# A four-attention chain in float32: one attention's query weights folded into its keys, masks and the maximum's subtraction on DVE, eps inside the statistics

## The reference, cut to what matters

```
x = block0(x): layernorm, attention with 8 heads of 32, residual; layernorm, U = (.. @ W_in.T + b_in) @ B
               s = silu(s @ A.T) + u_t over the 1024 rows; x += states @ C; x += mod
x = block1(x): qn = layernorm(x)*g + b;  q = qn @ wq + bq;  k, v = layernorm(ctx) @ wkv + bkv   (16 heads of 64)
               attn = softmax(causal(q k^T / 8));  x = attn v @ wo + bo + x
x = block2(x): q = x @ Wq.T + bq; scores = q k^T / 4                                            (16 heads of 16)
               scores = where(mask == 0, -1e9, scores); e = exp(scores - max) * mask
               probs = e / (sum(e) + 1e-9); x = layernorm(probs v @ Wo.T + bo + x)
x = block3(x): layernorm, scores = where(xa_mask, -float_max, q k^T / 4), softmax, @ v, proj    (16 heads of 16)
               x += attention; x += gelu(layernorm(x) @ fc1 + b) @ fc2 + b
```

## Time and profile before

| | |
|---|---|
| median of 3 runs | 1515.07 us (1514.07 to 1515.09) |
| the profiled execution | 1518.26 us, its span 1516.3 us |
| granted TensorE clock, mean | 0.984 |
| PE, PEld | 1438.1 us (95%), 1238.9 us (82%) |
| DVE | 954.2 us (63%) |
| ACT | 678.0 us (45%) |
| POOL | 451.6 us (30%) |

### The profile page before, as it was taken

How to read it: one execution, slowest core, us unless ns; L and a number is a source line. 1 busy time by engine, 2 the same in 40 slices (tenths; PEclk the granted TensorE clock), 3 DMA queues, 4 the chain that set the end, 5 groups by cost and what they waited for, 6 DMA issues and landing times.

```text
span 1516.3 us, 25350 instructions
## 1 busy us (share of the span) xinstructions
PE 1438.1 (95%) x9947; PEld 1238.9 (82%) x9947; DVE 954.2 (63%) x2220; ACT 678.0 (45%) x1507; POOL 451.6 (30%) x755
## 2 busy tenths in 40 slices
PE   6897888999999999999999999999999999899999
PEld 5776777888789879888897898878986998699778
DVE  4776664088756766586658627775677557747772
ACT  3554655523444344534454552345434443453443
POOL 4365442021431232134123311151115212420341
PEclk9999999899999999999999999999999999999999
DMA  3151233020000000000000001000000000000000
GB/s 94 46 115 45 82 82 114 1 75 1 1 16 8 8 2 15 15 1 7 9 15 1 8 15 16 2 1 8 22 1 1 15 15 1 1 15 15 1 1 14
DMA packets 46738, 34.22 MB, mean 23 GB/s; under 512 B 21981, under 2 KB 45340, under 8 KB 46108
## 3 DMA queue, kind: packets, MB, share of 16 engines
q1 hardware_dynamic: 46571, 32.59, 7.7%
q10 hardware_dynamic: 48, 0.01, 0.0%
HBM read 23.26 MB, written 8.39 MB: 21 GB/s over the span
## 4 chain that ended last, share of the span: by engine, by line
PE 85%; DVE 6%; ACT 4%; POOL 3%; issue 1%; DMA 1%; ACTq 0%; SPq 0%; DVEq 0%; POOLq 0%
PE ps L697 13%; PE ps L772 10%; PE ps L769 9%; PE ps L814 8%; PE ps L748 8%; PE ps L822 7%; PE ps L729 7%; PE ps L782 5%; PE ps L733 4%; PE ps L681 4%; PE ps L739 3%; PE ps L894 2%; PE ps L912 1%; DVE mx L1179 1%; ACT pr L1012 1%
## 5 line engine op out<-in xcount | busy, mean ns | idle before, releaser
L1391 POOL TENSOR_SCALAR rstd<-mv 128x1 f32<-128x1 f32 x192 | 43.1, 225 | 635.0 <-DVE mv L1152 634.2
L1012 ACT ACTIVATE pr<-pr 128x616 f32<-128x616 f32 x224 | 159.7, 716 | 156.5 <-DVE pr L1189 106.3
L1179 DVE TENSOR_REDUCE mx<-ps 128x8 f32<-128x616 f32 x224 | 178.0, 795 | 81.2 <-PE ps L739 47.5
L1016 ACT ACTIVATE pr<-ps 128x512 f32<-128x512 f32 x224 | 131.9, 595 | 189.7 <-PE ps L748 189.2
L991 ACT ACTIVATE tt<-ps,cols 128x128 f32<-128x128 f32 x320 | 127.5, 455 | 161.7 <-PE ps L681 160.7
L1248 DVE TENSOR_TENSOR xt<-xt,ps 128x256 f32<-128x256 f32 x192 | 79.9, 418 | 163.6 <-PE ps L822 83.0
L748 PE MATMUL ps<-ident,pr 128*128 128x128 f32 (+1 forms) x1120 | 162.4, 279 | 9.8 <-ACT pr L1012 5.6
L697 PE MATMUL ps<-tt,wq 128*128 128x128 f32 x1280 | 158.9, 278 | 2.7 <-ACT tt L991 2.5
L772 PEld LDWEIGHTS ps<-vtab,pr 128*128 128x128 f32 (+1 forms) x1280 | 153.5, 192 | 9.6 <-ACT pr L1016 7.3
L697 PEld LDWEIGHTS ps<-tt,wq 128*128 128x128 f32 x1280 | 152.2, 194 | 6.9 <-ACT tt L991 4.3
L772 PE MATMUL ps<-vtab,pr 128*128 128x34 f32 (+2 forms) x1280 | 153.8, 271 | 4.0 <-ACT pr L1016 3.5
(11 more groups left out here) (182 smaller groups left out, 2302.4 us busy)
## 6 DMA issues: line engine op xcount, KB each, us to landing
out_dram<-xt SPq DMA_DIRECT2D x64, 128.0 KB, 1.7
xt<-in_x_dram SPq DMA_DIRECT2D x32, 128.0 KB, 2.3
xt<-out_dram SPq DMA_DIRECT2D x32, 128.0 KB, 2.1
fc<-in_L_xattn_fc_w_dram SPq DMA_DIRECT2D x2, 1024.0 KB, 6.9
big<-in_L_xattn_wkv_dram SPq DMA_DIRECT2D x1, 2048.0 KB, 11.3
front<-in_L_xattn_wkv_dram SPq DMA_DIRECT2D x1, 2048.0 KB, 7.9
wo<-in_L_xattn_wo_dram SPq DMA_DIRECT2D x1, 1024.0 KB, 5.7
wq<-in_L_xattn_wq_dram SPq DMA_DIRECT2D x1, 1024.0 KB, 4.9
```

The lines of the kernel that those rows point to most:

```text
L1012: ac(v, v, ACT.Exp, scale=-ATTN[key[0]].scale).then_inc(done["expo"], 1)
L1016: ac(pr[:, run.lane, 0:4 * P], bank(run.lane, 0), ACT.Copy).then_inc(done["pturn_main"], 1)
L1179: v.tensor_reduce(mx[:, run.lane, :], score_view(run.lane), AX.X, ALU.max).then_inc(done["rowmax"], 1)
```

## The change

Five things are changed together, and the written order of all engines with them.

1. `L1`: the query is not made any more. A table `wk` [256 x 16 heads x 77 keys] for each batch of the pair takes its place: (layernorm gain and query weights) x keys, made by PE once per pair (`wk_mm`) and copied by DVE (`wk_sb`). Gain, bias `b` and `bq` go into it: the normalized row has its first column dropped (the columns sum to zero) and a column of ones added. The scores of a group are then four matmuls of 308 columns, two for each bank. The weights are prepared once (`fold` on POOL, `wqt_mm` on PE, `wqt_sb` on ACT). `query_add` is gone for this attention, and its `turned` is one plain copy of 256 columns.
2. `L2`, `L3`: PE adds no masks. DVE reads the scores from PSUM, adds the mask (`L3`, from the bytes of the mask) or takes the minimum with a bound (`L2`), and writes to `pr` (`bound`); `rowmax` reads `pr`, and `below` subtracts in SBUF. Two DVE steps become three.
3. eps times 256 stands as a third statistic in `stat`, so `aggr` gives var + eps, and `vareps` is gone.
4. POOL makes `mul2` and a `bound2`, and not `neg3`, nor the zeros of `kblk1`.
5. `big` is halved; the first half of the MLP's hidden columns goes into `pr`. The pair-0 value tables `vtw` have room for both groups.

```diff
 def norm_steps(key):
-    return [("stats", key), ("aggr", key), ("vareps", key), ("rstd", key), ("norm", key)]
+    return [("stats", key), ("aggr", key), ("rstd", key), ("norm", key)]
 def attention_steps(a):
-    if a is L1:
-        steps = [("query", "1a"), ("query", "1b"), ("query_add", "1a"), ("query_add", "1b")]
+    steps = [] if a is L1 else [("query", a.name), ("query_bias", a.name)]
...
-        steps += [("scores", k), ("rowmax", k), ("shift", k), ("expo", k)]
+        steps += [("scores", k)]
+        steps += [("bound", k), ("rowmax", k), ("below", k)] if a in (L2, L3) else [("rowmax", k), ("shift", k)]
 TURNS = {
     "tensor": (
-        "1010132031210310213002322312101301010201321013031030232120301231231301202013101301032032213210230131320310201212"
+        "0101023130013010121200213213210320210121303210100121323230310302020123211010321302320212310123013232102301013210301"
...
             def scores(key, run):
+                if a is L1:
+                    for k in range(2):
+                        h0 = (g * HG + k * HB) * KEYS
+                        for kc in range(KC):
+                            last = mm(bank(lane, k)[:, SFROM[k]:SFROM[k] + HB * KEYS], t[:, lane, kc, :], wk[:, kc, b, h0:h0 + HB * KEYS],
+                                      start=kc == 0, stop=kc == KC - 1 and run.tile > 0, skip_group_check=True)
...
-                if masked:
-                    m = {"1": causal[:, :, :], "2": neg2[:, run.tile:run.tile + 1, :],
-                         "3": neg3[:, run.batch, run.tile:run.tile + 1, :]}[a.name]
-                    for k in range(2):
-                        last = mm(bank(lane, k)[:, SFROM[k]:SFROM[k] + HB * KEYS], identb[:, :], m.to_broadcast([P, HB, KEYS]),
-                                  start=False, stop=True, skip_group_check=True)
+            def wqt_mm(key, run):
...
+                for kc in range(KC):
+                    last = mm(bk[:, 0:H], wq1[:, kc, c * P:(c + 1) * P], fold1[:, kc, :], start=kc == 0, stop=kc == KC - 1)
+            def wk_mm(key, run):
...
+                for n, c in enumerate(WK_PARTS[part]):
+                    for k in range(2):
+                        half = slice(k * P // 2, (k + 1) * P // 2)
+                        last = mm(item_bank("wk_mm", key, pair, k)[:, n * PK:(n + 1) * PK], wqT[half, c, ec * P:(ec + 1) * P],
+                                  kT[c // GC][half, c % GC, :], start=True, stop=True)
-            def query_add(key, run):
+            def bound(key, run):
+                dve.wait_ge(done["scores"], at("scores", key, run))
...
+                if key[0] == "2":
+                    top = bound2[:, run.tile:run.tile + 1, :].to_broadcast([P, HG, KEYS])
+                    last = v.tensor_tensor(heads_view(run.lane), score_view(run.lane), top, ALU.min)
+                else:
+                    off = out3[:, run.batch, run.tile:run.tile + 1, :].to_broadcast([P, HG, KEYS])
+                    last = v.scalar_tensor_tensor(heads_view(run.lane), off, NEG, score_view(run.lane), ALU.mult, ALU.add)
+            def below(key, run):
+                dve.wait_ge(done["rowmax"], at("rowmax", key, run))
+                top = mx[:, run.lane, :].unsqueeze(2).to_broadcast([P, HG, KEYS])
+                v.tensor_tensor(heads_view(run.lane), top, heads_view(run.lane), ALU.subtract).then_inc(done["below"], 1)
+            def wk_sb(key, run):
...
+                for k in range(2):
+                    o = wk[:, ec, :, :].rearrange("p b (c k n) -> p b c k n", k=2, n=KEYS)[:, :, c0:c0 + n, k, :]
+                    src = item_bank("wk_mm", key, pair, k)[:, 0:n * PK].rearrange("p (c b n) -> p b c n", c=n, b=PAIR)
+                    last = v.tensor_copy(o, src)
-            def vareps(key, run):
             def do_rstd(key, run):
-                pool.wait_ge(done["vareps"], at("vareps", key, run))
+                pool.wait_ge(done["aggr"], at("aggr", key, run))
             def do_masks(key, run):
...
-                    made(p.tensor_scalar(neg3[:, :, :, :], m3raw, NEG, None, ALU.mult))
...
+                made(p.tensor_scalar(bound2[:, :, :], mul2[:, :, :], 0.0, NEG, ALU.is_equal, ALU.mult))
+                p.tensor_scalar(bound2[:, :, :], bound2[:, :, :], -NEG, -1e9 / L2.scale, ALU.add, ALU.add).then_inc(done["masks"], 1)
```

More of the change, by code:

```diff
@@ L120, in table_steps @@
     p = str(pair)
-    steps = [] if pair else ([("v0_lay", p)] + [("weights_get", i) for i in range(LOADS)] + [("wkv1_get", p), ("masks", "2"), ("masks", "3")])
+    steps = [] if pair else ([("v0_lay", p)] + [("weights_get", i) for i in range(LOADS)] + [("wkv1_get", p), ("masks", "2")])
     if pair == 0:
@@ L124, in table_steps @@
             steps += [("w2_mm", str(i)), ("w2_sb", str(i))]
+        steps += [("fold", "1")]
+        for c in range(L1.chunks):
+            steps += [("wqt_mm", str(c)), ("wqt_sb", str(c))]
     else:
@@ L129, in table_steps @@
         steps += [("k_mm", f"{p}1{c}"), ("k1_sb", f"{p}1{c}")]
-    for g in range(L1.groups):
-        for c in range(GC):
-            steps += [("vt_mm", f"{p}{g}{c}"), ("vt_sb", f"{p}{g}{c}")]
-        for b in range(PAIR):
-            for j in range(TILES):
-                steps += [("vwo_mm", f"{p}{g}{b}{j}"), ("vwo_sb", f"{p}{g}{b}{j}")]
+    folded = []
+    for ec in range(KC):
+        for part in range(3):
+            folded += [("wk_mm", f"{p}{ec}{part}"), ("wk_sb", f"{p}{ec}{part}")]
+    values = [[(s, f"{p}{g}{c}") for c in range(GC) for s in ("vt_mm", "vt_sb")] for g in range(L1.groups)]
+    products = [[(s, f"{p}{g}{b}{j}") for b in range(PAIR) for j in range(TILES) for s in ("vwo_mm", "vwo_sb")] for g in range(L1.groups)]
+    if pair == 0:
+        steps += values[0] + values[1] + folded + products[0] + products[1]
+    else:
+        steps += folded + values[0] + products[0] + values[1] + products[1]
     for a in (L2, L3):
@@ L156 @@
     "tensor": ("turn", "query", "scores", "pturn", "mix", "proj", "uproj", "ssm", "fc1", "fc2",
-               "w2_mm", "k_mm", "vt_mm", "vwo_mm", "v_mm", "scan_u", "scan_r", "gap_turn", "more_pe"),
-    "scalar": ("turned", "query_bias", "expo", "pturn_main", "u_sb", "gelu", "w2_sb", "k1_sb", "vt_sb", "silu", "more_act"),
-    "vector": ("stats", "aggr", "norm", "query_add", "rowmax", "shift", "rowsum", "den_eps", "recip", "weigh",
-               "pturn_rest", "heads", "resid", "resume", "vwo_sb", "k_sb", "v_sb", "ends", "gap", "agree", "states"),
-    "gpsimd": ("vareps", "rstd", "prebias", "keep", "maskmul", "gain", "offset", "masks", "vtw_zero"),
+               "w2_mm", "wqt_mm", "k_mm", "wk_mm", "vt_mm", "vwo_mm", "v_mm", "scan_u", "scan_r", "gap_turn", "more_pe"),
+    "scalar": ("turned", "query_bias", "expo", "pturn_main", "u_sb", "gelu", "w2_sb", "wqt_sb", "k1_sb", "vt_sb", "silu", "more_act"),
+    "vector": ("stats", "aggr", "norm", "bound", "rowmax", "below", "shift", "rowsum", "den_eps", "recip", "weigh",
+               "pturn_rest", "heads", "resid", "resume", "wk_sb", "vwo_sb", "k_sb", "v_sb", "ends", "gap", "agree", "states"),
+    "gpsimd": ("rstd", "prebias", "keep", "maskmul", "gain", "offset", "masks", "fold", "vtw_zero"),
     "sync": ("load", "put", "get", "store", "weights_get", "wkv1_get", "v0_lay", "v_lay")}
@@ L239, in in_turn, with places @@
     assert all(at[c] == len(own[c]) for c in PLANS), engine
+    return out
+RING = ((2, 3, 4, 5, 6, 7), (0, 1, 2, 3))
+WK_PARTS = ((0, 1, 2), (3, 4, 5), (6, 7))
+def places(pair):
+    out, n = {}, 0
+    for s, k in table_steps(pair):
+        if s.endswith("_mm"):
+            n += n % 2 if s == "wk_mm" else 0
+            out[s, k] = n
+            n += 2 if s == "wk_mm" else 1
     return out
@@ L417, in xattn_chain @@
         mm_no = {it: n + 1 for n, it in enumerate(ITEMS)}
-        RING = ((2, 3, 4, 5, 6, 7), (0, 1, 2, 3))
-        EMPTIES = {"w2_mm": "w2_sb", "vt_mm": "vt_sb", "vwo_mm": "vwo_sb", "v_mm": "v_sb"}
-        TMM = [[(s, k) for s, k in table_steps(pair) if s.endswith("_mm")] for pair in range(2)]
+        EMPTIES = {"w2_mm": "w2_sb", "wqt_mm": "wqt_sb", "wk_mm": "wk_sb", "vt_mm": "vt_sb", "vwo_mm": "vwo_sb", "v_mm": "v_sb"}
+        PLACES = [places(pair) for pair in range(2)]
         def emptied(step, key):
@@ L706, in scores @@
                     if a is L1:
[L707 to L708 removed]
+                        pe.wait_ge(done["turned"], at("turned", "1", run))
                     else:
```

366 lines of the change are left out of this document (199 added, 167 removed).

## The result

The changed kernel took **1533.53 us** (median of 18 runs, 1520.12 to 1543.08); the kernel before, run beside it, 1516.96 (18 runs, 1511.02 to 1528.22). The ratio is 1.0083, with a 95% interval from 1.0053 to 1.0112: 0.8% slower, where 4.2% faster was forecast. The longest of the 18, over 1.5% above the shortest, counts as a slow run and is left out of the ratio; without it the median is 1533.22 us. The medians alone stand 1.1% apart, so a difference of medians here is good to some 3 or 4 us.

What follows compares the result with a forecast made beforehand. The prediction took PE to bound the kernel, busy 95% of the span, with DVE next in phase 1. Its terms took 1518.3 us to 1455.0, less 3.2: about 1452 us; own range 1435 to 1470, 80% range 1412 to 1492.

Steps and rivals of the forecast that it cites:

- signs that the prediction named: Listed checks: PE instruction count, step prices, DVE busy time, PE share, phase 1 length, largest POOL piece near 105 us.
- length of phase 1: Phase 1 of a pair was to take 525 to 545 us in place of 560 and 590.
- folding, tables, epsilon, stall, table loads: L1 query -113.7, wider scores +63.5, new PE tables +18.6, scan-end stall -3.9, POOL tables -3, vareps -5.4, ACT loads +3 us.
- masks leave PE: L2 and L3 in phase 1: 256 mask matmuls at 185 ns go, 47.4 us counted in full.
- bounds come on DVE: Phase 1: DVE gains net 66.8 us of work; +25 us taken on the path, between 0 and 46.
- PE waits for little: Phase 1: PE is busy 97 to 98%, so its -97.6 us of query, masks and scores counts in full.
- rival D: Removing masks and query pays nothing, as PE's short steps only filled its waits: 1515 +- 3 us; chance 0.03.
- waits for DVE: Phase 1: chain time on DVE, 91 us, grows as DVE's idle share falls from 33 to 22%; +25 us taken.
- rival B: DVE's waits grow more than its idle share says: +58 in place of +25 us, so 1485 us; chance 0.20.
- Rival C: DVE becomes the bound in phase 1: slower, 1621 us, if its share stays below about 73%; chance 0.07.
- weight loads don't set the pace: PE's matmul time follows columns: 128 and 256 columns, one load each, cost 111 and 216 ns; no term rests on it.
- small terms: Among them: vareps gone -5.4 us, stall at the scan's end -3.9, mask tables on POOL -3.

Runs made afterwards that it cites:

- searched orders: Phase 1 orders from a search over a replay of each kernel's trace: before 1509.5 us, changed 1512.5 and 1500.5, changed with masks back on PE 1470.9.
- zeros added there: Changed kernel with the 256 mask matmuls put back on PE as adds of zero, DVE's bounds kept: 1545.0 us, ratio 1.0180.
- the fastest kernel: Changed kernel with the L2 and L3 masks back on PE and a searched order of phase 1: 1470.9 us, ratio 0.9685 to the kernel before.

## Why the prediction was wrong

The prices of single steps were right, and almost all signs that the prediction named came out: 1120 instructions less, 260 ns for the wide scores, 0.79 and 0.87 us on DVE, DVE at 1020 us and 67% (1035 and 71% forecast), 2.32 us for the largest new POOL piece, now at 116 us (under 3 forecast), PE at 93% (93 to 95). What failed is the length of phase 1, about 560 and 594 us (932 to 1526) in place of 525 to 545, and with it the sum. By parts, in us:

| part | forecast | in the change's order | in searched orders |
|---|---|---|---|
| folding, tables, epsilon, stall, table loads | -41 | +2.6 | -38.6 |
| masks leave PE | -47.4 | -17 (of the kernel before) | -18.3 |
| bounds come on DVE | +25 | +30 (estimate) | +48 to +60 |
| all | -63 | +15.6 | -9.0 to +3.0 |

(The first row is -113.7 + 63.5 + 18.6 - 3.9 - 3 - 5.4 + 3. Measured: 1520.5 - 1517.9; 1470.9 - 1509.5. Second row: the kernels without masks. Nobody left the masks out in the change's order, so its -17 is taken from the kernel before, and the +30 that hangs on it is an estimate; zeros added there cost 11.5, which would make it +25. Third row: 1533.5 - 1520.5 + 17; 1500.5 or 1512.5 less 1452.7.)

**The step that failed** is "PE waits for little. Hence I count it in full, and put what is late next into the terms for waits". A busy share of 97 to 98% says that PE is seldom idle, not that taking work away from it brings the end nearer. Two kernels give 0.36 and 0.39 of a mask matmul's time. That the next step in the written order isn't ready any earlier is the likely reason; the runs show only the share. The masks alone make 30 of the 80 us between forecast and result. So nearly two thirds of the masks' time went as in rival D (the steps only filled PE's waits), to which I gave 0.03.

**The folding** made 44 more. The forecast's sum for it was met to 3 us (-41 against -38.6), but only between two orders that were both chosen for their kernels. That closeness is luck in part: the searches are good to some 12 us, a mask in the same order paid only 0.39 of its length, and the 43.8 us of `query_add` on DVE, which go with the query, were in the forecast's waits and not in this sum. How the 38.6 us divide isn't shown. In the order that came with the change the folding brought nothing. I took the change's order as given and asked of it only what stands where. A written order is a set of guesses on who is ready when; steps that grow from 136 to 260 ns a matmul, and others that vanish, can make them stale. What in the change's order loses the 40 us isn't shown: it wasn't tried with the folded kernel in the order of before, whose tables have other banks.

**The waits for DVE** were sized about right in the change's order (+25 against an estimated 25 to 30); DVE's part of the chain went from 91 to 137 us, the upper end of my range. In a tight order they cost 48 to 60 us for 101 us of bounds, as rival B priced them (+58), and more than the 18 that PE saves: the masks are better on PE in every order tried. Rival C named the outcome, slower, and its sign: DVE's share of phase 1 reached 70% (802.2 of 1140 us), under its 73%. Its mechanism isn't borne out. With the masks back on PE in the same order DVE has 63% (708.5 of 1133) and the time is 13 us less, where C had about 100.

**The clock** was no term at all, and no rival. Of the 80 us it has about 33: the changed kernel runs 104 us longer at 1.2 GHz than the kernel before (147 against 43), at 0.32 each. That is an estimate, since the price is the slope over 18 runs. It isn't a part beside the others, but lies in all measured rows above: the folded kernel with the masks on PE had 73 us there, in its new order 35. Summed over PE's steps of phase 1 in the two profiled executions, the time above a step's usual length is 55.0 us after and 8.3 before, so 47 us of the busy time that didn't go. The Trainium skill, "TensorE: Matmul & The Clock Gate", section Terms, puts the loss at the time at the lower level times one half; for the 104 us that would be 52, an estimate by that page. PE's steps agree with it: in the two stretches PE was at the lower level for some 115 us after (clock 0.97 and 0.93) and some 17 before, and 47 is about half of the difference. The time of the whole kernel doesn't, with 0.32 in place of 0.5; that part of the loss falls into waits is likely and not shown. Waits and clock may feed each other: from 1155 us PE waits in a stretch at full clock, and then does its transposes in 1.33 instead of 0.55 us. The order in time is shown, the cause isn't.

The claim that weight loads don't set the pace, on which no term rested, holds (260 ns with one load each). The small terms held in part where they can be seen: epsilon -5.3; at the scan's end the stall isn't gone, four ACT pieces of 0.4 us are left from 296.6 us, as the one shown, in place of 3.9 us; and where GpSimd makes the mask table, now from 115 to 121 us, PE is busy 11.48 of the 14 us from 112, in place of 9.73 of 14, so 1.8 us more, against 3 forecast.

## What to carry to other kernels

Where engines follow a written order, ask of a matmul that goes not how long it is, but what stands behind it and whether that is ready; test it by leaving the work out, which costs one run and gave 0.36 and 0.39 here. Judge a change that alters the lengths of steps with an order remade for it, and remake the order of the kernel before too: the same folding was worth 0 and 39 us. And when PE loses work but not busy time, look at its granted clock first.

## What the runs showed of the hardware

- The clock fell in a kernel whose PE was busy 93% of the span, in stretches such as 1140 to 1170 us, with PE busy 22.72 of 30. Its longest single wait there was 2.1 us, and in the 13 us ahead of the fall at about 1165 us it was busy 9.90.
- Executions of one program differ by 23 us (1520.12 to 1543.08), and the clock goes along with nearly all of it (correlation -0.98); the five runs of the fastest kernel, at 0.987 to 0.990, lie within 6 us (1468.15 to 1473.89).
- 64 matmuls of no use made a kernel 14 us faster by the medians and 11 by the ratios, with zeros as with weights; 128 of them gave nothing clear of noise.
- One clock level down, the steps of PE lost about half of the time spent there (47 of some 98 us), and the kernel 0.32 of it.
